# Writing the router's transposed rows to memory and reading them back as the operand of the shared expert's first six units

## The chip, the cores and the metric

One core of a Trainium2 chip runs the whole kernel in one launch. The metric is the device time in microseconds of that launch; several runs are taken and the median counts. The engines are TensorE (PE in the profile, with PEld for its weight loads), VectorE (DVE), ScalarE (ACT), GpSimd (POOL), and SyncE (SP), which only issues transfers here.

## The reference

An adaLN transformer block on x of 2 x 1024 tokens of width 512, all in float32: attention with 16 heads, then a feed-forward part. Only the second half matters here:

```python
h = _layernorm(x, axis=-1) * (1 + cb) + sb
x = x + gb * ffn(h)

def ffn(h):                                    # h: 2048 rows of 512
    topk_idx, topk_w = _route(h, router_weight, e_bias)   # logits = h @ router_weight.T, 8 of 64 experts
    moe_out = _moe_experts(h, topk_idx, topk_w, w_gate, w_up, w_down)
    return moe_out + silu(h @ sh_gate) * (h @ sh_up) @ sh_down
```

Each of the 64 experts takes up to 512/2 = 256 rows, and every row also passes the shared expert.

## The kernel before

The rows are held as 16 tiles of 128 tokens. Attention runs in chunks of two tiles. Behind each chunk, tile by tile, comes the residual and the second layer norm, whose result h (tile `h2`, two buffers) is stored to the table `h2_dram` by SP (line 592); PE transposes it (`turn`, L1189), ACT copies the transposed tile from PSUM into `h2T` (`rows_T`, L858), and PE multiplies `h2T` with the router's weights (`logits`, L1195). DVE then computes the routing in 33 small steps (`route`), and a position table by one-hot products: `hot` (L1784) and `collect` (L1793) on DVE, `weigh` on ACT (L880), `place` on PE (L1228). When all 16 tiles are placed, `finish_slots` writes the tile `slots` (L1801).

The feed-forward part is a list of units of 256 rows: six units of the shared expert in front (FRONT = 6, tiles 0 to 11), then the 64 experts, then the last two shared units. Every unit goes through the same stages:

- load of its 256 rows into one of three buffers `xg`: for shared units by SP from `h2_dram` (`load_shared`, L577), for experts by an indirect DMA of GpSimd with `slots` (`gather`, L715);
- `turn_rows` (L1314): eight PE transposes of `xg` into PSUM banks 0 and 1;
- `rows_hi` on ACT (L937): the float32r high part `x_hi` out of PSUM; `rows_lo` on DVE (L1812): the low part `x_lo`, PSUM minus `x_hi`;
- `up_first`, `up_second`, `up_third` on PE (L1328). `up_first` wants `x_hi`, `up_second` wants `x_lo`;
- `gates` on ACT (L942, L943), `hidden` on DVE (L1888, L1889), `hidden_hi` on ACT (L948, L950), `hidden_lo` on DVE (L1894, L1895), `down` on PE (L1367);
- for a shared unit `shared_out` on DVE adds the result to the residual (L1926); for an expert ACT and DVE weigh the rows and GpSimd adds them to a table in memory by indirect DMA (`add_rows`, L730).

Each engine's order is written out by hand; an engine runs its own list strictly in order and waits on semaphores. Between the end of attention and the experts' loop, DVE's list interleaves the six shared units with `route(4, n)` for the last two tiles, the last four `hot`/`collect` steps and `finish_slots`. PE's list holds `turn_shared(0)` to `turn_shared(5)` there, `up_first(2..4)` wait for `hidden` of the unit before (the first five units share PSUM banks), `up(5)` is followed by `turn_rows` of expert 0 (which waits for its gather), and from then on the loop is the same eight groups per expert.

Of the kernel before, what the change touches and what calls it, by code (L numbers as in the profile page):

```python
# [7 lines left out]
P = 128  # L8
# [3 lines left out]
KC = D // P  # L12
# [3 lines left out]
CAP = 2 * 1024 * TOPK // E  # L16
HALVES = CAP // P
# [7 lines left out]
FRONT = 6  # L25
# [3 lines left out]
RING = 3  # L29
# [30 lines left out]
def build_program(nc, x, c_t, wmod, wq_t, wkv_t, wo_t, w_pre, w_qn, w_kn, router_t, e_bias,  # L60
# [7 lines left out]
    acc_dram = [nc.dram_tensor(f"acc_dram{p}", [NTOK + EXTRA, D], f32).ap() for p in range(2)]  # L68
    rows_dram = nc.dram_tensor("rows_dram", [B, 4 * D], f32).ap()

    ctx = ExitStack()
    with ctx:
        def sem(name):
            return ctx.enter_context(nc.semaphore(name))
# [165 lines left out]
        def pair(n):  # L240
            return ps[:, 2 * n:2 * n + 2, :]
# [18 lines left out]
        s_wq, s_wkv, s_late = sem("s_wq"), sem("s_wkv"), sem("s_late")  # L260
        s_h2_out = [sem(f"s_h2_out{p}") for p in range(2)]
        s_wts, s_wts_out = sem("s_wts"), sem("s_wts_out")
        s_sh_w = sem("s_sh_w")
# [72 lines left out]
        def tile_rows(t):  # L336

            return row_view(h2_dram, t - t % TPF, TPF)[:, 0, t % TPF, 0:D]
# [169 lines left out]
        def tile_due(m, part, steps=1):  # L508
# [8 lines left out]
            return found  # L517

        def gate_bank(n, p):

            return 0 if isinstance(n, int) and n < EARLY else p
# [5 lines left out]
        def _(sp):  # L527
# [41 lines left out]
            for p in range(2):  # L569
                sp.dma_start(acc_dram[p].rearrange("(t p) n -> p t n", p=P),  # L570
                             zeros[:, 0:D].unsqueeze(1).to_broadcast([P, (NTOK + EXTRA) // P, D])).then_inc(s_init, 16)

            def load_shared(n, at):
                for p in range(2):
                    sp.wait_ge(s_h2_out[p], 16 * (n + 1))
                for h in range(HALVES):
                    sp.dma_start(xg[at % RING][:, h, 0:D], tile_rows(n * HALVES + h))\  # L577
                      .then_inc(s_xg[at % RING], 16)

            for t in range(CT * CLOSE):  # L580
                if t == CT * (CLOSE - 1):
                    sp.wait_ge(s_mm, pieces_before(NT))
                    sp.wait_ge(s_sc, 2 * steps_before(CLOSE))
                    for b in range(B):
                        sp.dma_start(gb[:, b, :], rows_dram[b, 3 * D:4 * D].unsqueeze(0).to_broadcast([P, D])).then_inc(s_gb, 16)
                    sp.dma_start(sh_gu[:, :, :], sh_gate_up).then_inc(s_sh_w, 16)
                    sp.dma_start(sh_d[:, 0, :], sh_down[0:IA, :]).then_inc(s_sh_w, 16)
                    sp.dma_start(sh_d[0:IB, 1, :], sh_down[IA:EI, :]).then_inc(s_sh_w, 16)
                    for n in range(RING):
                        load_shared(n, n)  # L590
                sp.wait_ge(s_h2, t + 1)
                sp.dma_start(tile_rows(t), h2[:, t % 2, :]).then_inc(s_h2_out[t % 2], 16)
                if t % RT == 0 and t:
                    store_weights(t // RT - 1)
# [12 lines left out]
            sp.wait_ge(s_sc, 2 * steps_before(NCHUNK))  # L607
            sp.wait_ge(s_T, RING)
            load_shared(RING, RING)
            sp.wait_ge(s_pv, steps_before(NCHUNK) // 2)  # L610
# [4 lines left out]
            for n in range(RING + 1, FRONT):  # L615
                sp.wait_ge(s_T, n)
                load_shared(n, n)
            begin, n = ROUTES[NR - 1]
# [34 lines left out]
        def _(pool):  # L653
# [30 lines left out]
            def row_rms(q):  # L684
                pool.wait_ge(s_oms, q + 1)
                inv_sqrt(orstd[:, q % 2, :], oms[:, :], CT).then_inc(s_orstd, 1)

            for m in range(FIRST * H, END):
                for q, g, kt in steps_at(m):
                    if kt >= keys(q) - CT:  # L690
                        causal(q, g, kt)
                for q in chunk_due(m, "row_rms"):
                    row_rms(q)
                for tile, _ in tile_due(m, "rstd"):
                    tile_rstd(tile)
                for tile, _ in due(m, "head_rms"):
                    head_rms(tile)
                for k, at in enumerate(STATS_AT, 2):
                    if m == at + STATS[k][1] - STATS[k][0] + 1:
                        tiles_rstd(k)  # L700
            row_rms(CLOSE)
            for t in (CT * CLOSE, CT * CLOSE + 1):
                tile_rstd(t)
            for p in range(2):
                pool.wait_ge(s_h2_out[p], 16 * (NT // 2))
# [27 lines left out]

            for e in range(RING + 1):
                gather(e)
# [7 lines left out]
        def _(act):  # L743
# [284 lines left out]
        def _(pe):  # L1028
# [273 lines left out]

            pe.sem_inc(s_T, 2)
            pe.sem_inc(s_gu, 2)
# [77 lines left out]

            def turn_shared(n):
                turn_rows(n, n % RING, s_xg, n // RING + 1)

            a, b = CT * CLOSE, CT * CLOSE + 1
            turn_shared(0)
            pe.wait_ge(s_ex, a)
# [12 lines left out]
            up_third(0, 0, sh_gu_hi, sh_gu_lo)  # L1401
            turn_shared(1)
            turn(b)
# [3 lines left out]
            up_third(1, 1, sh_gu_hi, sh_gu_lo)  # L1407
            turn_shared(2)
# [4 lines left out]
            turn_shared(3)  # L1413
            down(1, 1, sh_d_hi[0], sh_d_lo[0])
            up(3, 1, sh_gu_hi, sh_gu_lo)
            turn_shared(4)
            down(2, 0, sh_d_hi[0], sh_d_lo[0])
# [4 lines left out]
            up_third(4, 0, sh_gu_hi, sh_gu_lo)  # L1422
            turn_shared(5)
            place(15)
# [60 lines left out]
        def _(dve):  # L1485
# [429 lines left out]
            def step(n, p, expert=None, r=None):  # L1915
                hidden(n + 1, 1 - p)
                if expert is not None:
                    take_weights(expert, r)
                rows_lo(n + 2, p)
                hidden_lo(n + 1, 1 - p)  # L1920
# [9 lines left out]
            divide(CLOSE, NG - 1)  # L1930
            rows_lo(0, 0)
            hot(12, 0)
# [17 lines left out]
            hidden(0, 0)  # L1950
            rows_lo(1, 1)
            hidden_lo(0, 0)
# [7 lines left out]
            for n in range(18, COUNTED):  # L1960
                route(4, n)
            rows_lo(3, 1)
            for n in range(COUNTED, 28):
# [7 lines left out]
            hot(14, 1)  # L1971
            rows_lo(4, 0)
            shared_out(2, 2)
# [6 lines left out]
            finish_slots()  # L1980
            rows_lo(5, 1)
            hidden_lo(4, 0)
# [123 lines left out]
```

## Time and profile before

| | |
|---|---|
| median of 3 runs | 1230.19 us |
| lowest, highest | 1229.79, 1232.54 us |
| span of the profiled execution | 1233.0 us |
| busy PE / DVE / ACT / POOL | 95% / 79% / 62% / 40% |
| share of the chain that ended last, on PE | 71% |

The profiled execution's span is 2.8 us above the median. Its times stand in microseconds from the span's start. The attention part ends near 645, the six shared units in front run to 708, the experts to about 1184, and the rest is the last shared units and the final sums. Within the profile a line of code is named L1314 and so on; a busy time says how long an engine had an instruction at hand, and the bracket behind a row says how long it had been idle before, and whose result ended the idle time.

### The profile page before, as it was taken

Reading aid. Unit: us, or ns where it says so; the run is one execution under the profiler, and the core shown is the slowest. Engines: PE = TensorE matmul, PEld = TensorE weight load, DVE = VectorE, ACT = ScalarE, POOL = GpSimd, SP = SyncE. Lnnn points to the kernel's source line nnn. Section 1 sums busy time; section 2 is a strip of 40 time slices with the busy share of each in tenths; the row PEclk is TensorE's granted clock in tenths of the full one; section 3 lists DMA queues with packets and bytes.
Section 4 is the critical chain, followed back from the end, with each engine's and each line's share of the span. In section 5 each row is a group of like instructions: output and inputs, shape, how many; then the busy total and the mean of one; then the engine's idle time right before and its main releaser. Section 6 shows DMA issues by size and latency. Waiting matters only on the chain.

```text
span 1233.0 us, 25541 instructions
## 1 busy us (share of the span) xinstructions
PE 1168.1 (95%) x8905; PEld 879.7 (71%) x8905; DVE 972.6 (79%) x1881; ACT 762.0 (62%) x1507; POOL 497.9 (40%) x375
## 2 busy tenths in 40 slices
PE   8988999999999988999999999999999999999996
PEld 4455556555565655555557899999999999999982
DVE  4678776756657888775767889899888999999976
ACT  3456555555664644455564477787777887777841
POOL 1122212102122111201100148887888778788740
PEclk9999999989999998999999999999999999999999
DMA  9570000000000000003004179999999999999988
GB/s 349 172 302 1 2 18 2 10 9 2 15 10 10 9 1 22 1 10 95 29 14 141 25 225 299 289 302 302 292 295 306 299 297 296 298 301 294 298 231 290
DMA packets 75167, 189.95 MB, mean 154 GB/s; under 512 B 11544, under 2 KB 12184, under 8 KB 74832
## 3 DMA queue, kind: packets, MB, share of 16 engines
q1 hardware_dynamic: 44704, 116.27, 28.0%
q0 software_dynamic: 28672, 71.32, 23.5%
q10 hardware_dynamic: 1712, 1.32, 0.3%
q8 instruction: 48, 0.79, 0.3%
q14 instruction: 31, 0.25, 0.1%
HBM read 136.36 MB, written 52.51 MB: 153 GB/s over the span
## 4 chain that ended last, share of the span: by engine, by line
PE 71%; DVE 13%; DVEq 4%; issue 3%; DMA 3%; ACT 3%; POOL 0%; SPq 0%; POOLq 0%; ACTq 0%
PE ps L1328 22%; PE ps L1367 12%; PE ps L1147 8%; PE ps L1314 5%; PE ps L1177 4%; PE ps L1132 4%; PE ps L1060 4%; PE ps L1092 4%; DVE nmax L1610 3%; PE ps L1117 2%; DMA acc_dram<-y,slots 1%; PE ps L1032 1%; PE ps L1164 1%; DMA wq<-in_wq_t 1%; PE ps L1195 1%
## 5 line engine op out<-in xcount | busy, mean ns | idle before, releaser
L730 POOL DMA_INDIRECT acc_dram<-y,slots x128 | 252.2, 1971 | 74.1 <-issue 47.9
L1610 DVE TENSOR_REDUCE nmax<-ps 128x1 f32<-128x512 f32 (+3 forms) x304 | 191.3, 656 | 95.3 <-PE ps L1096 52.4
L839 ACT ACTIVATE probs<-ps 128x512 f32<-128x512 f32 (+1 forms) x320 | 159.0, 554 | 87.2 <-PE ps L1132 86.3
L681 POOL TENSOR_SCALAR_AFFINE_SELECT probs<-probs 128x512 f32<-128x512 f32 x64 | 44.3, 691 | 376.7 <-ACT probs L839 376.6
L715 POOL DMA_INDIRECT xg<-h_dram,slots x128 | 130.7, 1021 | 84.4 <-DVE slots L1801 40.5
L1092 PE MATMUL ps<-kpad,qpT 128*128 128x512 f32 (+3 forms) x384 | 146.7, 450 | 15.5 <-DVE nmax L1610 13.4
L1328 PE MATMUL ps<-x_hi,e_gu_hi 128*112 128x256 f32 (+1 forms) x768 | 120.1, 278 | 0.0
L1132 PE MATMUL ps<-qT,kT 98*128 98x512 f32 (+1 forms) x320 | 115.1, 437 | 5.0 <-ACT probs L839 4.8
L1328 PE MATMUL ps<-x_hi,e_gu_lo 128*112 128x256 f32 (+1 forms) x768 | 119.6, 278 | 0.0
L1812 DVE TENSOR_TENSOR e_gu_lo<-e_gu,e_gu_hi 128x1408 fp32r<-128x1408 f32 x64 | 103.8, 1622 | 11.0 <-ACT e_gu_hi L960 9.9
L1328 PE MATMUL ps<-x_lo,e_gu_hi 128*112 128x256 f32 (+1 forms) x768 | 109.9, 279 | 0.0
L1328 PEld LDWEIGHTS ps<-x_hi,e_gu_hi 128*112 128x112 f32 (+1 forms) x768 | 105.7, 179 | 5.9
L1092 PEld LDWEIGHTS ps<-kpad,qpT 128*128 128x128 f32 x384 | 67.3, 195 | 50.3 <-DVE nmax L1610 25.4
L1328 PEld LDWEIGHTS ps<-x_hi,e_gu_lo 128*112 128x112 f32 (+1 forms) x768 | 100.8, 179 | 0.0
L1328 PEld LDWEIGHTS ps<-x_lo,e_gu_hi 128*112 128x112 f32 (+1 forms) x768 | 96.0, 179 | 0.0
L1812 DVE TENSOR_TENSOR x_lo<-ps,x_hi 128x1024 fp32r<-128x1024 f32 x72 | 88.1, 1224 | 2.9 <-ACT x_hi L937 1.9
L960 ACT ACTIVATE e_gu_hi<-e_gu 128x1408 fp32r<-128x1408 f32 x64 | 88.2, 1378 | 0.1
L1367 PE MATMUL ps<-e_d_hi,hid_hi 112*128 112x512 f32 (+1 forms) x256 | 85.9, 417 | 0.0
L937 ACT ACTIVATE x_hi<-ps 128x1024 fp32r<-128x1024 f32 x72 | 73.9, 1026 | 18.5 <-PE ps L1314 18.1
L1147 PE MATMUL ps<-probs,v_sb 128*32 128x256 f32 (+1 forms) x1280 | 83.4, 380 | 0.6 <-POOL probs L681 0.6
L1367 PE MATMUL ps<-e_d_hi,hid_lo 112*128 112x512 f32 (+1 forms) x256 | 80.8, 397 | 0.0
L1147 PE MATMUL ps<-probs,ones 128*32 128x256 f32 (+1 forms) x1280 | 79.4, 367 | 0.0
(238 smaller groups left out, 2375.1 us busy)
## 6 DMA issues: line engine op xcount, KB each, us to landing
e_gu<-in_gate_up SPq DMA_DIRECT2D x64, 704.0 KB, 7.3
e_d<-in_w_down SPq DMA_DIRECT2D x64, 224.0 KB, 4.7
acc_dram<-h SPq DMA_DIRECT2D x2, 4608.0 KB, 26.0
e_d<-in_w_down SPq DMA_DIRECT2D x64, 128.0 KB, 5.4
wmod_b<-in_wmod SPq DMA_DIRECT2D x2, 2048.0 KB, 22.0
xg<-h_dram SPq DMA_DIRECT2D x16, 256.0 KB, 7.0
acc_a<-acc_dram SPq DMA_DIRECT2D x8, 512.0 KB, 10.0
acc_b<-acc_dram SPq DMA_DIRECT2D x8, 512.0 KB, 7.7
```

The costliest lines, as they stand in the source:

```text
L715: pool.indirect_dma_start(out=xg[r][:, h, :], out_offset=None, in_=h2_dram, in_offset=bass.IndirectOffsetOnAxis(ap=slots[:, at:at + 1], ax ...
L730: pool.indirect_dma_start(out=acc_dram[a], out_offset=bass.IndirectOffsetOnAxis(ap=slots[:, at:at + 1], axis=0), in_=y[e % 2][:, h, :], in ...
L839: act.activation(probs[:, n % PROBS, 2 * pr:2 * pr + 2, off:CW], unit_bank(2 * n + pr)[:, :, off:CW], ACT.Exp).then_inc(s_exp, 1)
L937: act.activation(x_hi[p][:, :, :].rearrange(flat), pair(0).rearrange(flat), ACT.Copy).then_inc(s_xa, 1)
L960: act.activation(e_gu_hi[p][:, :, :].rearrange(flat), e_gu[p][:, :, :].rearrange(flat), ACT.Copy)\
L1092: last = pe.matmul(view[:, a, :], qpT[:, t % 2, (first + a) // GH, :], kpad[:, (first + a) % GH, lo:hi], start=(a == 0), stop=(a == heads ...
L1132: pe.matmul(unit_bank(2 * n + pr)[:, :, off:CW], kT[0:QK, b, kt * P:kt * P + P], qT[q % 2][0:QK, head:head + 2, off:CW], start=True, stop= ...
L1147: last = pe.matmul(ps[HD * j:HD * j + HD, PV_BANK, at + off:at + CW], v_sb[:, b, kt, :] if at == 0 else ones[:, :], probs[:, (n + kt % 2) ...
L1328: last = pe.matmul(dst, w[:, cc, col:col + wide], rows_t[:, cc, :], start=(k == 0 and cc == 0), stop=(k == 2 and cc == KC - 1))
L1367: last = pe.matmul(ps[:, 6 + h, :], left[:, h * P:(h + 1) * P], w, start=(k == 0), stop=(k == len(products) - 1))
L1610: dve.tensor_reduce(nmax[:, 1 if lo else 0, first:first + heads], max_view(n, heads, hi - lo), AX.X, ALU.max, negate=True).then_inc(s_max, 1)
L1812: return dve.tensor_tensor(dst[:, :, :].rearrange(flat), whole[:, :, :].rearrange(flat), hi[:, :, :].bitcast(f32).rearrange(flat), ALU.sub ...
```

## The change

A third table, `turned_dram`, holds the rows of the six front units already transposed. For tiles 0 to 11, SP writes `h2T` to it right behind the store of `h2`, and `rows_T` of the next tile waits until that store has landed. `load_shared` of the six front units becomes `load_turned`: the transposed rows land in the same `xg` buffers. PE's six `turn_shared` are gone. ACT's `rows_hi` reads the buffer instead of PSUM for these units, and the low parts, six `rows_lo` of DVE, become six `turned_lo` of GpSimd with both inputs in SBUF. `turned_lo(0)` stands in GpSimd's list ahead of the last `row_rms`; `turned_lo(1..4)` after the last `tile_rstd` and ahead of the waits for the gathers; `turned_lo(5)` after `gather(0)` and `gather(1)`.

```diff
+            def load_turned(n):
+                for p in range(2):
+                    sp.wait_ge(s_turned_out[p], 16 * (n + 1))
+                for k in range(0, KC, 2):
+                    sp.dma_start(turned(n)[:, k:k + 2, :], turned_dram[n, :, k:k + 2, :]).then_inc(s_xg[n % RING], 16)
...
                 sp.dma_start(tile_rows(t), h2[:, t % 2, :]).then_inc(s_h2_out[t % 2], 16)
+                if t < TURNED:
+                    sp.wait_ge(s_h2T, t + 1)
+                    half = slice(t % HALVES * P, t % HALVES * P + P)
+                    sp.dma_start(turned_dram[t // HALVES, :, :, half], h2T[:, :, :]).then_inc(s_turned_out[t % 2], 16)
...
-            sp.wait_ge(s_T, RING)
-            load_shared(RING, RING)
+            sp.wait_ge(s_xd, 1)
+            load_turned(RING)
...
             for n in range(RING + 1, FRONT):
-                sp.wait_ge(s_T, n)
-                load_shared(n, n)
+                sp.wait_ge(s_xd, n - RING + 1)
+                load_turned(n)
...
+            def turned_lo(n):
+                pool.wait_ge(s_xa, n + 1)
+                pool.tensor_tensor(x_lo[n % 2][:, :, :], turned(n), x_hi[n % 2][:, :, :].bitcast(f32),
+                                   ALU.subtract).then_inc(s_xd, 1)
+
+            turned_lo(0)
             row_rms(CLOSE)
             for t in (CT * CLOSE, CT * CLOSE + 1):
                 tile_rstd(t)
+            for n in range(1, FRONT - 1):
+                turned_lo(n)
...
-            for e in range(RING + 1):
+            gather(0)
+            gather(1)
+            turned_lo(FRONT - 1)
+            for e in range(2, RING + 1):
                 gather(e)
...
             def rows_T(t):
                 if t:
                     act.wait_ge(s_lg, t)
+                if 0 < t <= TURNED:
+                    act.wait_ge(s_turned_out[(t - 1) % 2], 16 * ((t - 1) // 2 + 1))
...
             def rows_hi(n, p):
                 hold(act, s_gu, n + 1)
-                act.wait_ge(s_T, n + 3)
-                act.activation(x_hi[p][:, :, :].rearrange(flat), pair(0).rearrange(flat), ACT.Copy).then_inc(s_xa, 1)
+                if in_front(n):
+                    act.wait_ge(s_xg[n % RING], 32 * (n // RING + 1))
+                    act.activation(x_hi[p][:, :, :].rearrange(flat), turned(n).rearrange(flat), ACT.Copy).then_inc(s_xa, 1)
+                else:
+                    act.wait_ge(s_T, n + 3)
+                    act.activation(x_hi[p][:, :, :].rearrange(flat), pair(0).rearrange(flat), ACT.Copy).then_inc(s_xa, 1)
...
-            turn_shared(0)
...
-            rows_lo(0, 0)
```

The other five `turn_shared` of PE and the other five `rows_lo` of DVE go in the same way, each from its place in the hand-written list.

## Rows read from the trace of the kernel before

**Rows 1.** Busy time by stretch: us, then PE, PEld, DVE, ACT, POOL, clock, DMA share, GB/s.

```profile
670.00:702.00 32.00, 29.33 (x210) 26.07 (x209) 26.93 (x84) 15.25 (x31) 0.00 (x0) 1.00 0.07 19
900.00:1100.00 200.00, 200.00 (x1469) 188.06 (x1468) 182.84 (x273) 158.13 (x272) 161.74 (x109) 1.00 1.06 298
```

**Rows 2.** Chain that ended last, in order of time: start, us, what.

```profile
701.83 0.30 DVE slots L1801
...
703.10 1.19 POOL xg L715
...
704.59 3.78 DMA xg<-h_dram,slots
```

**Rows 3.** VectorE in order of time: start, us, line, operation, idle before.

```profile
673.65 0.17 DVE L1704 TENSOR_TENSOR lo<-lo 128x16 f32<-128x16 f32 x1
...
675.69 1.22 DVE L1812 TENSOR_TENSOR x_lo<-ps,x_hi 128x1024 fp32r<-128x1024 f32 x1
...
683.14 0.29 DVE L1737 TENSOR_TENSOR wts<-score,sel 128x128 f32<-128x128 f32 x1
...
685.01 1.22 DVE L1812 TENSOR_TENSOR x_lo<-ps,x_hi 128x1024 fp32r<-128x1024 f32 x1
...
691.92 0.17 DVE L1770 SCALAR_TENSOR_TENSOR col<-key,top 128x16 f16<-128x16 f32 x1
...
697.26 0.29 DVE L1793 TENSOR_TENSOR found<-found,ps 128x128 f32<-128x128 f32 x1 [0.16 <-issue]
```

**Rows 4.** ScalarE in order of time.

```profile
672.42 1.01 ACT L937 ACTIVATE x_hi<-ps 128x1024 fp32r<-128x1024 f32 x1
...
676.02 0.83 ACT L950 ACTIVATE hid_hi<-hid 64x256 fp32r<-64x256 f32 x2
...
680.59 0.37 ACT L943 ACTIVATE gact_b<-ps 64x256 f32<-64x256 f32 x1
...
689.22 0.36 ACT L943 ACTIVATE gact_b<-ps 64x256 f32<-64x256 f32 x1
```

**Rows 5.** TensorE in order of time.

```profile
695.18 1.10 PE L1228 MATMUL ps<-hot_col,hot_row 128*128 128x128 f16 x8
696.03 1.17 PE L1328 MATMUL ps<-x_lo,sh_gu_hi 128*128 128x256 f32 x8
...
704.67 1.07 PE L1328 MATMUL ps<-x_lo,sh_gu_hi 128*128 128x256 f32 x8
...
708.51 1.06 PE L1314 MATMUL ps<-con,xg 128*128 128x128 f32 x8 [1.34 <-DMA xg<-h_dram,slots]
```

**Rows 6.** GpSimd in order of time, the fourth gather behind the slots.

```profile
708.30 0.95 POOL L715 DMA_INDIRECT xg<-h_dram,slots  x1 [0.30 <-issue]
```

**Rows 7.** GpSimd's groups over the whole span, shapes apart.

```profile
L681 POOL TENSOR_SCALAR_AFFINE_SELECT probs<-probs 128x512 f32<-128x512 f32 x64 | 44.3, 691 | 376.7 <-ACT probs L839 376.6
...
L663 POOL TENSOR_TENSOR center<-center,rstd 128x4 f32<-128x4 f32 x3 | 0.6, 200 | 0.4
```

**Rows 8.** GpSimd, then VectorE, in order of time near 320 us.

```profile
318.93 0.63 POOL L681 TENSOR_SCALAR_AFFINE_SELECT probs<-probs 128x512 f32<-128x512 f32 x1 [6.89 <-ACT probs L839]
...
320.39 3.24 POOL L655 TENSOR_TENSOR rr<-ms,mhalf 128x17 f32<-128x17 f32 x1
...
316.73 0.43 DVE L1757 SCALAR_TENSOR_TENSOR marked<-score,cmp_a 128x256 f32<-128x256 f32 x1
...
319.07 0.77 DVE L1759 TENSOR_TENSOR marked<-marked,con 128x256 f32<-128x256 f32 x1
...
320.62 0.74 DVE L1667 SCALAR_TENSOR_TENSOR h<-xres,mv,mods 128x512 f32<-128x512 f32 x1
```

**Rows 9.** TensorE by stretch: us, PE busy, granted clock, DMA share, GB/s.

```profile
637.00:640.00 3.00, 0.84 (x10) 0.97 0.00 0
640.00:642.00 2.00, 2.00 (x19) 0.50 0.00 0
```

**Rows 10.** Transfers by line over the span: count, KB each, median us to landing.

```profile
h_dram<-h SPq DMA_DIRECT2D x14, 256.0 KB, 2.0
```

More of the change, by code:

```diff
@@ L69, in build_program @@
     rows_dram = nc.dram_tensor("rows_dram", [B, 4 * D], f32).ap()
+    turned_dram = nc.dram_tensor("turned_dram", [FRONT, P, KC, CAP], f32).ap()
     ctx = ExitStack()
@@ L261, in build_program @@
         s_h2_out = [sem(f"s_h2_out{p}") for p in range(2)]
+        s_turned_out = [sem(f"s_turned_out{p}") for p in range(2)]
         s_wts, s_wts_out = sem("s_wts"), sem("s_wts_out")
@@ L517, in tile_due, with turned, in_front @@
             return found
+        TURNED = FRONT * HALVES
+        def turned(n):
+            whole = xg[n % RING][:, :, :].rearrange("p h n -> p (h n)")[:, 0:KC * CAP]
+            return whole.rearrange("p (c t) -> p c t", t=CAP)
+        def in_front(n):
+            return isinstance(n, int) and n < FRONT
         def gate_bank(n, p):
@@ L615, in _ @@
             for n in range(RING + 1, FRONT):
-                sp.wait_ge(s_T, n)
-                load_shared(n, n)
+                sp.wait_ge(s_xd, n - RING + 1)
+                load_turned(n)
             begin, n = ROUTES[NR - 1]
@@ L1301, in _ @@
                     logits(tile)
-            pe.sem_inc(s_T, 2)
+            pe.sem_inc(s_T, FRONT + 2)
             pe.sem_inc(s_gu, 2)
@@ L1381, in down_last @@
                 last.then_inc(s_dn, 1)
-            def turn_shared(n):
-                turn_rows(n, n % RING, s_xg, n // RING + 1)
             a, b = CT * CLOSE, CT * CLOSE + 1
-            turn_shared(0)
             pe.wait_ge(s_ex, a)
@@ L1401, in _ @@
             up_third(0, 0, sh_gu_hi, sh_gu_lo)
-            turn_shared(1)
             turn(b)
@@ L1407, in _ @@
             up_third(1, 1, sh_gu_hi, sh_gu_lo)
-            turn_shared(2)
             pe.wait_ge(s_found, 14)
@@ L1412, in _ @@
             count(4)
-            turn_shared(3)
             down(1, 1, sh_d_hi[0], sh_d_lo[0])
             up(3, 1, sh_gu_hi, sh_gu_lo)
-            turn_shared(4)
             down(2, 0, sh_d_hi[0], sh_d_lo[0])
@@ L1422, in _ @@
             up_third(4, 0, sh_gu_hi, sh_gu_lo)
-            turn_shared(5)
             place(15)
@@ L1918, in step @@
                     take_weights(expert, r)
-                rows_lo(n + 2, p)
+                if not in_front(n + 2):
+                    rows_lo(n + 2, p)
                 hidden_lo(n + 1, 1 - p)
@@ L1950, in _ @@
             hidden(0, 0)
-            rows_lo(1, 1)
             hidden_lo(0, 0)
@@ L1961, in _ @@
                 route(4, n)
-            rows_lo(3, 1)
             for n in range(COUNTED, 28):
@@ L1971, in _ @@
             hot(14, 1)
-            rows_lo(4, 0)
             shared_out(2, 2)
@@ L1980, in _ @@
             finish_slots()
-            rows_lo(5, 1)
             hidden_lo(4, 0)
```

## The prediction

> **What bounds the kernel now.** I read the busy time by stretch first, then the chain that ended last, then each engine in order of time. From 709 us to the last units PE has no gap: in a stretch of 200 us it is busy for 200.00 [rows 1]. Whatever moves the start of this stretch moves the end by as much. It starts with PE's transposes of expert 0 at 708.51, which waited for the gathered rows [rows 5]. The chain leads back from there to GpSimd's gather at 703.10 and to DVE's `slots`, which end at 702.13 [rows 2]. So two times matter: when `slots` is ready, and how long after it PE can turn expert 0, now 708.51 - 702.13 = 6.4 us. Before that, from 670 to 702, PE is busy for 26.07 by its loads and 29.33 by its matmuls, DVE for 26.93 of 32 us [rows 1]; the chain there is almost all DVE, its routing steps and the units' parts in one list. The question is not what PE's transposes cost, but what DVE's list gains and what happens behind `slots`.
>
> **Part by part. PE's transposes** (`turn_shared`): each has a step of about 0.9 us, but PE waited after or before most of them for `hidden` or `shared_out` of DVE. They are worth only what they free: ACT's `rows_hi(1)` need not wait for them, which starts the last tile's logits and so the routing some 0.3 us earlier. Taken as -0.3.
>
> **DVE loses three `x_lo` of 1.22 us between the start of routing and `slots`.** They are not worth the same. The first at 675.69 ran to 676.9 [rows 3], and the step behind it, `hidden_lo(1)`, wants ACT's `hid_hi`, which ended at 676.02 + 0.83 = 676.85 [rows 4]: removed, it leaves a wait in its place and gains 0. The second at 685.01 [rows 3] has a routing step behind it that waits for nothing: -1.2. The third (unit 4) stands between the one-hot products and `collect(14)`; see below. `x_lo(0)` and `x_lo(1)` lie before PE's out projection and ahead of an idle wait for the logits: 0. `x_lo(5)` stood just behind `slots`.
>
> **GpSimd's subtraction, 128x1024 with two inputs in SBUF.** No row shows it. DVE does it in 1.22 [rows 3]. GpSimd's one-input select of 128x512 takes 0.69, in the undisturbed case 0.63 [rows 7, 8], and a small two-input product 0.20 [rows 7]. That gives 0.43 per 512 elements above a fixed 0.20: 1.06 if the second input cost nothing, 1.9 with a second stream of inputs, and 2.5 if all of the select's 0.63 is counted four times. I take 1.9, since a second stream of the same length is the nearest that the rows support. The Trainium skill (GPSIMD Engine Reference, section "Performance versus the Vector engine") measures 4497 ns for the same kind of operation at 2048 elements, which as an estimate would be 2.25 us here; no run here shows it, and by it the forecast would be 1.0 to 1.5 us later.
>
> **What DVE pays for it.** Beside the select at 318.93 to 319.56, DVE's two-input step at 319.07 took 0.77, where the same width at 316.73 took 0.43 [rows 8]: it waited until GpSimd was through. Against it, DVE's step at 320.62 kept its 0.74 beside a GpSimd operation of 3.24 that reads only 17 elements [rows 8]. So the exclusion lasts as long as GpSimd reads, and 1024 elements are read for nearly the whole 1.9 us. The routing steps are small two-input steps, all from SBUF, so I follow each of the three:
> - `turned_lo(2)` starts when ACT's `x_hi` ends, 673.43 [rows 4], less the 0.3: 673.1. DVE stands then at the step of 673.65 [rows 3], a two-input one: it loses 1.9. Shift of DVE's list: -0.3 + 1.9 = +1.6.
> - `turned_lo(3)`: ACT's gates end at 680.96 [rows 4]; with the shift and 1.0 for `x_hi` the subtraction runs from 683.6 to 685.5. DVE reaches the two-input step of 683.14 [rows 3] at 684.7 and waits 0.7. Shift +2.3, and -1.2 for the removed `x_lo(3)`: +1.1.
> - `turned_lo(4)`: gates end at 689.58 [rows 4]; PE is still late by 1.6, so it runs from about 692.2 to 694.1. DVE reaches the step of 691.92 [rows 3] at 693.0 and waits 1.1: +2.2. With this shift `place(14)` on PE goes from 695.18 to 697.4; its successor came 0.85 later [rows 5], so `collect(14)` can run at 698.35 where it ran at 697.26 [rows 3]: +1.1. The removed `x_lo(4)` is what allows this. `place(15)` and `hidden(4)` follow with the same shift.
>
> `slots` is then ready at 702.13 + 1.1 = 703.2. The Trainium skill states this exclusion (SBUF — State Buffer, section "Who interferes with whom": a DVE instruction with two SBUF inputs contends with a GpSimd instruction that reads SBUF, and the second to issue blocks fully). It speaks against this change. By it, as by the row of 0.77, the slots are 1.1 later; without it they would be earlier by 2.2 (next part but one).
>
> **Behind `slots`: the step that decides.** `turned_lo(5)` is behind four gather issues in GpSimd's list. The fourth ended at 708.30 + 0.95 = 709.25 [rows 6], 7.1 us after `slots`. Then come the 0.3 that stands between two GpSimd instructions [rows 6], 1.9 for the subtraction and 0.1 for the handover: `x_lo(5)` is there 9.4 us after `slots`. PE has `up_first(5)` done by then and stands at `up_second(5)`. From there to the end of the unit's products it took 708.51 - 1.34 - 704.67 = 2.5 [rows 5]. So expert 0 is turned 11.9 us after `slots`, where it was 6.4: +5.5. The gathered rows, which ended the wait before, landed 704.59 + 3.78 - 702.13 = 6.2 us after `slots` [rows 2] and have long been there. Everything behind (gathers 2 and 3, `add_rows`) has experts of time.
>
> **The clock.** `up_second(5)` ran 704.67 - 702.13 = 2.5 us after `slots` [rows 5]; with 9.4 in its place PE idles some 6.9 us. After a gap of about 2 us (busy 0.84 of 3.00 from 637) the granted clock was 0.50 from 640 to 642 [rows 9], that is 1.2 instead of 2.4 GHz, with PE fully busy. I take that the same follows here and lasts about 3.4 us, a bit longer than this row: half of it is lost, +1.7; between 0 and 3.4.
>
> **The rest.** Twelve more stores of 256 KB in the attention part: a store lands in 2.0 us [rows 10], the next tile's `rows_T` comes many microseconds later, and the DMA engines are nearly idle there; 0, or up to 1 if the added waits in ACT's list cost 0.1 each. `turned_lo(0)` ahead of `row_rms`: the residual waits for PE's out projection anyway, 0. Loads of units 3 to 5 are asked for earlier than they were needed: 0.
>
> **Sum.** +1.1 (slots) + 5.5 (behind slots) + 1.7 (clock) = +8.3. Against the profiled span of 1233.0 that is 1241.3; the span is 2.8 above the median, and the difference goes to the median: 1230.2 + 8.3 = 1238.5 us.
>
> **Rivals.**
> - A, the above: 1238.5, between 1235.5 (subtraction 1.5, no clock loss) and 1241 (subtraction 2.25, more clock). Chance 0.55.
> - B, DVE isn't held by GpSimd. For it speaks the step of 0.74 beside the long operation [rows 8]. Then the list has only -0.3, 0, -1.2, and behind `place(14)`, which now is 1.5 earlier, another -0.7 because `x_lo(4)` is gone: slots -2.2, total -2.2 + 5.5 + 1.7 = +5.0, 1235.2; without clock loss 1233.5. Chance 0.2.
> - C, the other side, faster: GpSimd gives the gathers to its descriptor work and takes up the subtraction at once, so that `x_lo(5)` is ready before the gathered rows land. It decides from 6.4 - 2.5 = 3.9 us behind `slots`. Then only B's gain is left: -2.2, 1228.0. Against it: each GpSimd instruction started 0.30 after the last one's end [rows 6], none beside it. Chance 0.06.
> - D, worse: the subtraction takes 2.5 or more, as DVE and GpSimd hold each other, and the slow clock lasts 6.8 us. Slots +2.4, behind them +6.1, clock +3.4: +11.9, 1242.1. Chance 0.13.
> - E, C's overlap with A's losses on DVE, or the change hidden for another reason: about 1230. Chance 0.06.
>
> **How the numbers follow.** The likeliest is A, 1238.5. Range 1232.8 to 1242.5: it takes B whole, A whole, and most of D, and leaves C and E out. Faster by over 0.2% (2.5 us, about what a measurement of this kernel can tell from no change) is only a part of C: 0.04; within it are the rest of C, E and a little of B: 0.10; slower 0.86.
>
> **What would show it.** In the profile after: GpSimd's `x_lo` of five units with 1.5 to 2.3 us each, and DVE's two-input routing steps of 0.17 to 0.29 us lengthened to about 2 beside them (A) or not (B); `slots` near 703; PE idle for 6 to 7 us ahead of an L1328 row on `x_lo,sh_gu_hi`, released by POOL, and a clock of 0.50 behind it; turns of expert 0 near 715 to 717; all behind shifted by one constant. Wrong it would be if PE's wait ahead of that row were short: then GpSimd's order does not hold the subtraction back, and the sum loses its largest term.

## The result, and the profile after

The changed kernel takes 1241.15 us in the median (1237.56 to 1241.83). The ratio to the kernel before is 1.0075, with an interval of 1.0061 to 1.0089: slower by 9.2 us, between 7.5 and 11.0 (the two medians differ by 11.0). One further run of the kernel before took 2864.72 us, a slow one, and is in neither the ratio nor the profiles. The profiled execution took 1239.94 us, with a span of 1238.2. Forecast were 1238.5 us and a loss of 8.3 us, from two places: `slots` 1.1 later (1.4 if counted from the routing's first step, as below), and expert 0 turned 7.2 later behind them. The two places are right. The sizes are not: the first cost 4.0 and the second 6.5.

Its busy times over the whole span, from the first part of the page:

```profile
PE 1163.8 (94%) x8857; PEld 876.6 (71%) x8857; DVE 974.4 (79%) x1875; ACT 761.9 (62%) x1507; POOL 511.2 (41%) x381
```

GpSimd has gained 1 point of share and nothing stands out. The loss doesn't show in shares. By stretch of the new kernel (columns as in [rows 1]) it does:

```profile
670.00:702.00 32.00, 24.57 (x156) 22.17 (x155) 25.39 (x70) 11.35 (x25) 7.11 (x3) 0.89 0.06 19
709.00:720.00 11.00, 8.71 (x49) 8.27 (x50) 3.05 (x7) 3.98 (x7) 4.78 (x4) 0.71 0.49 160
900.00:1100.00 200.00, 200.00 (x1468) 188.06 (x1467) 182.44 (x272) 158.34 (x272) 161.59 (x109) 1.00 1.06 297
```

The expert part is as it was: 200.00 of 200 us on PE, as in [rows 1]. In the routing stretch PE has 4.8 us less of busy time, of which its four transposes (`turn_shared`, 1.03 to 1.07 us each, overlapping their neighbours) make some 4. The matmul clock is 0.89 where it was 1.00, and GpSimd, which did nothing there, is busy for 7.11 with three instructions. These are GpSimd's instructions in order of time (as [rows 6]; three subtractions, the first gathers, the last subtraction):

```profile
670.12 2.34 POOL L726 TENSOR_TENSOR x_lo<-xg,x_hi 128x1024 fp32r<-128x1024 f32 x1 [5.17 <-ACT x_hi L974]
682.19 2.41 POOL L726 TENSOR_TENSOR x_lo<-xg,x_hi 128x1024 fp32r<-128x1024 f32 x1 [9.73 <-ACT x_hi L974]
689.50 2.37 POOL L726 TENSOR_TENSOR x_lo<-xg,x_hi 128x1024 fp32r<-128x1024 f32 x1 [4.91 <-ACT x_hi L974]
703.64 1.19 POOL L746 DMA_INDIRECT xg<-h_dram,slots  x1 [11.77 <-DVE slots L1832]
705.13 0.97 POOL L746 DMA_INDIRECT xg<-h_dram,slots  x1 [0.30 <-issue]
706.41 1.20 POOL L746 DMA_INDIRECT xg<-h_dram,slots  x1 [0.30 <-issue]
707.92 0.95 POOL L746 DMA_INDIRECT xg<-h_dram,slots  x1 [0.30 <-issue]
708.89 2.35 POOL L726 TENSOR_TENSOR x_lo<-xg,x_hi 128x1024 fp32r<-128x1024 f32 x1
```

A subtraction takes 2.34 to 2.41 us, not 1.9. The last one starts only when the fourth gather is issued. VectorE beside them, to be held against [rows 3]:

```profile
667.16 0.23 DVE L1718 TENSOR_SCALAR biased<-ex 128x128 f32<-128x128 f32 x1 [1.60 <-ACT ex L902]
...
670.22 2.26 DVE L1735 TENSOR_TENSOR lo<-lo 128x16 f32<-128x16 f32 x1
...
675.64 0.43 DVE L1925 TENSOR_TENSOR hid_lo<-hid,hid_hi 112x256 fp32r<-112x256 f32 x1 [1.21 <-ACT hid_hi L990]
...
682.21 2.53 DVE L1768 TENSOR_TENSOR wts<-score,sel 128x128 f32<-128x128 f32 x1
...
691.35 0.55 DVE L1797 TENSOR_SCALAR top<-key 128x16 f32<-128x16 f32 x1 [0.43 <-issue]
...
697.65 0.29 DVE L1824 TENSOR_TENSOR found<-found,ps 128x128 f32<-128x128 f32 x1 [1.37 <-PE ps L1268]
...
702.37 0.29 DVE L1832 SCALAR_TENSOR_TENSOR slots<-found,spare 128x128 int32<-128x128 f32 x1
...
705.14 1.65 DVE L1843 TENSOR_TENSOR e_gu_lo<-e_gu,e_gu_hi 128x1408 fp32r<-128x1408 f32 x1 [0.26 <-issue]
```

The step that took 0.17 at 673.65 [rows 3] takes 2.26, and the one that took 0.29 at 683.14 [rows 3] takes 2.53. Each ends where the subtraction beside it ends (672.46 and 684.60; the steps at 672.48 and 684.74). Such a step is called held below: it ends only when GpSimd's instruction has. TensorE, to be held against [rows 5]:

```profile
674.48 1.22 PE L1368 MATMUL ps<-x_hi,sh_gu_hi 128*128 128x256 f32 x4 [4.20 <-DVE hid L1920]
...
690.58 0.74 PE L1407 MATMUL ps<-sh_d_hi,hid_hi 112*128 112x512 f32 x2 [2.78 <-DVE xres L1958]
...
711.29 2.08 PE L1368 MATMUL ps<-x_lo,sh_gu_hi 128*128 128x256 f32 x8 [6.07 <-POOL x_lo L726]
...
715.56 1.03 PE L1354 MATMUL ps<-con,xg 128*128 128x128 f32 x8
```

PE has three long waits, 4.20, 2.78 and 6.07 us. The same eight products that took 1.07 in [rows 5] take 2.08 after the last wait. The granted clock says why; PE by stretch in the new kernel (us, PE busy, clock, DMA share, GB/s):

```profile
674.70:678.10 3.40, 3.40 (x18) 0.54 0.14 53
691.80:695.20 3.40, 3.40 (x13) 0.55 0.01 2
703.00:708.80 5.80, 2.22 (x18) 0.98 0.43 118
709.00:715.70 6.70, 4.41 (x22) 0.53 0.78 257
```

Behind each of the three waits there is a stretch at half clock (1.2 instead of 2.4 GHz), two of 3.4 us and one that covers what is left of unit 5. The kernel before has none between 645 and 709.

**Where the time went**, with the end of the routing's first step (`biased<-ex`) as a mark: 670.83 before (its row starts at 670.60 and takes 0.23) and 667.39 after.

| us | before | after | difference |
|---|---|---|---|
| first routing step ends | 670.83 | 667.39 | -3.44 |
| from there to the end of `slots` | 31.29 | 35.27 | +3.98 |
| from `slots` to expert 0 turned on PE | 6.39 | 12.90 | +6.51 |
| sum: expert 0 turned | 708.51 | 715.56 | +7.05 |

Of the -3.44, 3.2 arose in the attention part: its last marker, DVE's `sel_b`, ended at 639.79 before and at 636.58 after. Experiment 4 speaks against these 3.2 belonging to the change. From that marker to the turn of expert 0 the change costs 10.3 us, which lies inside the interval of the timed runs. The 7.05 by which the experts start later is kept to the final sums, whose first product on PE starts at 1208.53 against 1201.50. The span shows only 5.2 of it, because the profile of before took 10.7 us from PE's last product to its end, this one 8.9, and the experiments' 8.8 to 10. The distances between the marks repeat better than the spans do: experiment 4 leaves this part as it was and has 31.32 and 6.41 us for the second and third line of the table.

### The profile page after: what moved, and what is told of

Its sections match the earlier page's. It is cut to its first block, busy times and chain, and to the rows that moved or that the text cites. A ratio compares the mean times of both kernels' runs of the same rounds, so it can differ in the third digit from the quotient of the medians.

```text
span 1238.2 us, 25451 instructions
## 1 busy us (share of the span) xinstructions
PE 1163.8 (94%) x8857; PEld 876.6 (71%) x8857; DVE 974.4 (79%) x1875; ACT 761.9 (62%) x1507; POOL 511.2 (41%) x381
## 4 chain that ended last, share of the span: by engine, by line
PE 73%; DVE 13%; DVEq 4%; issue 3%; ACT 3%; DMA 2%; POOL 1%; SPq 0%; POOLq 0%; ACTq 0%
PE ps L1368 23%; PE ps L1407 13%; PE ps L1187 8%; PE ps L1354 5%; PE ps L1217 4%; PE ps L1100 4%; PE ps L1172 4%; PE ps L1132 4%; DVE nmax L1641 3%; PE ps L1157 2%; PE ps L1072 1%; PE ps L1204 1%; DMA wq<-in_wq_t 1%; PE ps L1235 1%; ACT probs L873 1%
## 5 line engine op out<-in xcount | busy, mean ns | idle before, releaser
L1843 DVE TENSOR_TENSOR x_lo<-ps,x_hi 128x1024 fp32r<-128x1024 f32 x66 | 80.8, 1225 | 1.5 <-ACT x_hi L977 0.7
L982 ACT ACTIVATE gact_a<-ps 112x256 f32<-112x256 f32 x72 | 27.7, 384 | 88.2 <-PE ps L1368 88.2
```

Of the source, the lines that this page charges most:

```text
L1843: return dve.tensor_tensor(dst[:, :, :].rearrange(flat), whole[:, :, :].rearrange(flat), hi[:, :, :].bitcast(f32).rearrange(flat), ALU.sub ...
```

## The experiments

My theory: the loss has two causes that add up. GpSimd's place for unit 5, behind four gather issues, costs expert 0 its start; GpSimd's reading beside DVE's two-input steps costs the routing. Against it stood: that GpSimd's slowness alone is the cause (no exclusion), that the new stores to memory cost time, and that only the wait behind `slots` counts.

**Experiment 1: unit 5's subtraction ahead of the wait for `slots`.**

```diff
-            for n in range(1, FRONT - 1):
+            for n in range(1, FRONT):
                 turned_lo(n)
...
-            gather(0)
-            gather(1)
-            turned_lo(FRONT - 1)
-            for e in range(2, RING + 1):
+            for e in range(RING + 1):
                 gather(e)
```

> The changed kernel with one step moved: GpSimd's low part of unit 5 stands ahead of the waits for the slots, no longer behind four gather issues. Theory (the recorded prediction's largest term is GpSimd's order): the wait of 6.1 us ahead of up_second(5) goes, and the slow clock behind it; expert 0 is turned 6.4 to 7.5 us after the slots instead of 12.9, so the whole is 5.5 to 6.5 us faster than the changed kernel, about 1234. Rival (DVE's lost time in the routing is the main term, the wait merely absorbs it): under 2 us gained, still about 1239. GpSimd takes the subtraction at 701.5 to 703.9, so the first gather may start 0.3 later.

Measured: 1240.05 us (1239.07 to 1242.60), ratio 1.0066 (1.0041 to 1.0091). PE's wait ahead of `up_second(5)` is gone, and still almost nothing is won. The time is the rival's (about 1239), but not for the rival's reason. Its GpSimd, then DVE, then PE:

```profile
703.49 2.41 POOL L726 TENSOR_TENSOR x_lo<-xg,x_hi 128x1024 fp32r<-128x1024 f32 x1 [9.56 <-ACT x_hi L971]
...
708.89 2.30 POOL L746 DMA_INDIRECT xg<-h_dram,slots  x1 [0.30 <-issue]
...
703.90 2.15 DVE L1827 SCALAR_TENSOR_TENSOR spare<-found,spare 128x128 f32<-128x128 f32 x1
...
708.72 1.62 DVE L1840 TENSOR_TENSOR e_gu_lo<-e_gu,e_gu_hi 128x1408 fp32r<-128x1408 f32 x1 [0.26 <-issue]
...
706.96 1.07 PE L1365 MATMUL ps<-x_lo,sh_gu_hi 128*128 128x256 f32 x8
...
715.46 1.94 PE L1351 MATMUL ps<-con,xg 128*128 128x128 f32 x8 [6.01 <-DMA xg<-h_dram,slots]
```

The subtraction now runs while DVE makes `spare`, the step ahead of `slots`: 2.15 us instead of 0.29. So `slots` end 36.96 us behind the first routing step (35.27 in the changed kernel). Then the second gather's issue falls beside DVE's `e_gu_lo` and takes 2.30 instead of 0.97, and expert 0 is turned 9.0 behind `slots`. PE's wait is only moved, from `x_lo` to the gathered rows, and is 6.01 long; the products behind it are slow again (1.94 us instead of 1.06). From the routing's first step to the turn of expert 0, 46.0 us pass, against 48.2 in the changed kernel and 37.7 before. My expectation missed since I had placed this subtraction in a free time of DVE.

**Experiment 2: all six low parts on DVE, at the places where the kernel before has them, read from the loaded rows.** GpSimd has none; PE's transposes stay away, the stores stay in.

```diff
-            turned_lo(0)
...
-            for n in range(1, FRONT - 1):
-                turned_lo(n)
...
             def rows_lo(n, p):
+                if in_front(n):
...
+                    dve.wait_ge(s_xa, n + 1)
+                    dve.wait_ge(s_xd, n)
+                    dve.tensor_tensor(x_lo[p][:, :, :], turned(n), x_hi[p][:, :, :].bitcast(f32), ALU.subtract).then_inc(s_xd, 1)
+                    return
```

> The changed kernel, but all six low parts are made by DVE at the places of the kernel before, with both inputs in SBUF; GpSimd makes none. Transposes stay removed. Theory (both losses come from GpSimd: the exclusion in the routing and its order behind the slots): DVE's routing steps are back at 0.17 to 0.29 us, slots come 31.2 to 31.5 us after the routing's first step (35.5 in the changed kernel), expert 0 is turned 6.4 us behind the slots; total 1229 to 1230.5, like the kernel before or up to 1 us faster. Rival (removing PE's transposes, reading x_hi from SBUF, or the stores cost the time): over 1233.

Measured: 1229.08 us (1227.49 to 1232.90), ratio 0.9983 (0.9968 to 0.9998); a second time, beside other runs of before, 1228.93, ratio 0.9987 (0.9971 to 1.0003), where a ratio of 0.998 to 0.9995 was expected. The whole loss is gone. DVE there, around the place of the held step:

```profile
670.41 0.18 DVE L1730 TENSOR_TENSOR lo<-lo 128x16 f32<-128x16 f32 x1
...
672.45 1.21 DVE L1912 TENSOR_TENSOR x_lo<-xg,x_hi 128x1024 fp32r<-128x1024 f32 x1
673.74 0.42 DVE L1927 TENSOR_TENSOR hid_lo<-hid,hid_hi 112x256 fp32r<-112x256 f32 x1
```

The step is short again. The subtraction from SBUF takes DVE 1.21, as from PSUM [rows 3], and `hidden_lo(1)` follows without a wait: this subtraction costs nothing, as the prediction had it, for in the changed kernel the same `hid_lo` waits 1.21 for ACT's `hid_hi` (675.64, above). `slots` come 30.92 behind the first step and the turn 6.46 behind `slots`; before it was 31.29 and 6.39, and the second profile of this kernel has 30.91 and 6.47. So the rows from memory, without PE's transposes, are worth 0.4 us ahead of `slots`; the timed runs alone hardly tell this gain from none.

**Experiment 3: unit 5 alone back to DVE, behind `slots`; units 0 to 4 on GpSimd.** The `rows_lo` of experiment 2, for n = 5 only, and the gathers in one loop.

> The changed kernel, but DVE makes the low part of unit 5 right behind the slots, as the kernel before; GpSimd makes units 0 to 4. Theory: the same gain as with GpSimd's step moved ahead: no wait of PE behind the slots, 5.5 to 6.5 us off the changed kernel, and what is left over the kernel before, 3 to 4.5 us, is the exclusion in the routing: 1233 to 1235. Rival (no exclusion, the long steps of 2.26 and 2.53 in the trace are something else and would be hidden): 1229 to 1231.

Measured: 1235.07 us (1232.33 to 1236.86), ratio 1.0028 (1.0016 to 1.0040), at the upper end of what was expected. `slots` to turn: 6.4, as before. First step to `slots`: 35.11, as in the changed kernel. Its DVE:

```profile
669.58 2.26 DVE L1735 TENSOR_TENSOR lo<-lo 128x16 f32<-128x16 f32 x1
...
681.46 2.53 DVE L1768 TENSOR_TENSOR wts<-score,sel 128x128 f32<-128x128 f32 x1
...
690.59 0.65 DVE L1797 TENSOR_SCALAR top<-key 128x16 f32<-128x16 f32 x1 [0.42 <-issue]
```

The same three steps are held. The two causes are apart now: the one behind `slots` is worth the way from this kernel to the changed one, 1.0075 - 1.0028, some 5.8 us; the one ahead of `slots` the way from experiment 2 to this kernel, 1.0028 - 0.9983, some 5.5 us. By the intervals each is uncertain by some 2 us. By the profiles it is 6.5 and 4.2 (35.11 - 30.92).

**Experiment 4: the kernel before with the changed kernel's stores and ACT's waits for them, and nothing else.** What is stored is read by nobody.

```diff
+                if t < TURNED:
+                    sp.wait_ge(s_h2T, t + 1)
+                    half = slice(t % HALVES * P, t % HALVES * P + P)
+                    sp.dma_start(turned_dram[t // HALVES, :, :, half], h2T[:, :, :]).then_inc(s_turned_out[t % 2], 16)
```

> The kernel before with one part of the change alone: the transposed rows of tiles 0 to 11 are also stored to memory, and ACT's copy of the next tile waits for the store; nothing reads them. Theory: 0, at most 1 us, since the stores land in 2 us on idle transfer engines: 1229.5 to 1231. Rival: each store or the wait delays ACT in attention, or shifts where the clock falls: 1232 or more, or 1228 or less, with the attention part longer or shorter in the trace (in the changed kernel's profile it was 3.2 us shorter).

Measured: 1232.09 us (1229.38 to 1233.41), ratio 1.0001 (0.9988 to 1.0013). The stores cost nothing that shows within 1.5 us. The median alone lies in the rival's band, but the runs of before beside it had 1231.03. Its profiled execution reached the marker `sel_b` at 636.28, 3.5 us earlier than the profile of before, while the timed runs don't differ. The ten profiles of kernels with these stores besides it have this marker between 636.0 and 638.7, without a change to the attention part among them. So about 3 us of this part vary from one execution to another, and the profile of before is a long one; what makes them vary stays open, and there is only one profile without the stores.

**Experiment 5: unit 2's subtraction done twice on GpSimd**, to weigh the exclusion by itself.

```diff
+                if n == 2:
+                    pool.tensor_tensor(x_lo[n % 2][:, :, :], turned(n), x_hi[n % 2][:, :, :].bitcast(f32), ALU.subtract)
+                    pool.drain()
```

> The changed kernel with GpSimd's low part of unit 2 computed twice, one after the other (the first has no reader). Theory (a GpSimd operation that reads two tiles from SBUF holds DVE's two-input steps for as long as it runs): the long step of 2.26 us at the routing's twelfth instruction stays, and a second DVE step, the next one or the one after it, is lengthened to about 2.3 us too, so hidden(1) and the slots come about 2.2 us later than in the changed kernel (37.5 to 38 us behind the routing's first step, against 35.5). Rival (the 2.26 is a delay of its own kind, such as a semaphore or an instruction fetch at this place): one long step only, slots unchanged.

Measured: 1241.88 us, one run. GpSimd, then DVE:

```profile
669.69 2.34 POOL L727 TENSOR_TENSOR x_lo<-xg,x_hi 128x1024 fp32r<-128x1024 f32 x1 [5.17 <-ACT x_hi L977]
672.17 2.34 POOL L729 TENSOR_TENSOR x_lo<-xg,x_hi 128x1024 fp32r<-128x1024 f32 x1
...
669.80 2.26 DVE L1738 TENSOR_TENSOR lo<-lo 128x16 f32<-128x16 f32 x1
672.13 0.18 DVE L1740 TENSOR_TENSOR lo<-lo,mid 128x16 f32<-128x16 f32 x1
672.38 2.16 DVE L1742 TENSOR_TENSOR gsum<-hi,lo 128x16 f32<-128x16 f32 x1
```

Two subtractions, two held steps, and one DVE step, begun in the 0.14 us between them, keeps its usual 0.18. `slots` come 36.56 behind the first step, 1.3 later than in the changed kernel instead of the 2.2 to 2.7 that I expected: the later subtractions then meet DVE elsewhere, and not all of a held step reaches `slots`.

**Experiment 6: two fills of `x_lo` by GpSimd ahead of unit 2's subtraction.** Is it GpSimd's being busy that holds DVE, or its reading?

```diff
+                if n == 2:
+                    for _ in range(2):
+                        pool.memset(x_lo[n % 2][:, :, :].bitcast(f32), 0.0)
+                        pool.drain()
```

> The changed kernel with two memsets of the same tile by GpSimd, 0.95 us each as the kernel before has one, right ahead of its low part of unit 2, which then starts about 2.2 us later. Theory (it is GpSimd's reads that hold DVE): beside the memsets DVE's two-input steps keep their 0.17 to 0.29 us, and the long step appears only when the subtraction begins, further on in the routing or at hidden_lo. Rival (any GpSimd instruction on SBUF holds DVE, writes too): steps of 0.9 us and more already beside the memsets.

Measured: 1238.85 us, one run. GpSimd (the two fills in one row), then DVE:

```profile
669.54 2.03 POOL L728 MEMSET x_lo<- 128x1024 f32 x2 [5.16 <-ACT x_hi L978]
671.71 2.39 POOL L730 TENSOR_TENSOR x_lo<-xg,x_hi 128x1024 fp32r<-128x1024 f32 x1
...
669.66 0.18 DVE L1739 TENSOR_TENSOR lo<-lo 128x16 f32<-128x16 f32 x1
...
672.99 1.39 DVE L1929 TENSOR_TENSOR hid_lo<-hid,hid_hi 112x256 fp32r<-112x256 f32 x1 [1.22 <-ACT hid_hi L994]
```

Beside the fills, DVE's two-input step keeps 0.18. Beside the subtraction that follows, `hid_lo` takes 1.39 instead of 0.43 and ends 0.3 behind it (674.38 and 674.10). So neither GpSimd's being busy nor its writes hold DVE. What the subtraction has and the fills lack is reads from SBUF, and the exclusion goes with them. One run doesn't tell this kernel's time from the changed one's.

**Experiment 7: experiment 2 with units 3 and 4 on GpSimd**, where DVE was said to lose least and gain 1.2 twice. Edit: `rows_lo` returns for n in (3, 4), and GpSimd has `turned_lo(3)` and `turned_lo(4)`.

> The version in which DVE makes the front units' low parts, but GpSimd makes those of units 3 and 4, the two that stood in DVE's way: each removes 1.22 us from DVE's list. Theory (exclusion by the remaining GpSimd time): each costs DVE's next two-input step 1.0 to 1.2 us, so the two nearly cancel; within 0.5 us of the version with all on DVE, 1228.6 to 1229.6, slots 30.7 to 31.7 us behind the routing's first step against 31.2. Rival (only the long step in unit 2 mattered, the others are free): 1.5 to 2 us faster than it, about 1227.

Measured: 1231.16 us (1229.61 to 1234.76), ratio 1.0011 (0.9998 to 1.0023), against 0.9983 of experiment 2: by the ratios some 3 us lost, by the medians 2, with intervals that just touch, where I expected a tie. GpSimd, then DVE:

```profile
680.06 2.39 POOL L727 TENSOR_TENSOR x_lo<-xg,x_hi 128x1024 fp32r<-128x1024 f32 x1 [19.07 <-ACT x_hi L971]
688.93 2.38 POOL L727 TENSOR_TENSOR x_lo<-xg,x_hi 128x1024 fp32r<-128x1024 f32 x1 [6.49 <-ACT x_hi L971]
...
681.47 1.13 DVE L1765 TENSOR_TENSOR wts<-score,sel 128x128 f32<-128x128 f32 x1
...
689.10 2.25 DVE L1796 TENSOR_SCALAR top<-top 128x16 f32<-128x16 f32 x1
```

The second held step reads one array only, 128x16, and takes 2.25 us. It ends with the subtraction (691.35 and 691.31). My rule for DVE, two inputs in SBUF, was too narrow. Unit 4's subtraction met such a step early in its 2.38 us, and the PE that waits for it then was at half clock: `slots` 33.35 behind the first step, 2.4 later than in experiment 2.

**Experiment 8: the changed kernel, with matmuls that fill PE's three waits** (17, 10 and 25 products of a constant array, 128x512, into a bank of PSUM that nobody reads then). It tells what the clock costs by itself.

```diff
+            def fill(k):
+                for _ in range(k):
+                    pe.matmul(ps[:, 0, :].rearrange("p (a k) -> p a k", k=P), ones_b[:, :], ones_b[:, :].unsqueeze(1).to_broadcast([P, 4, P]), start=True, stop=True)
...
+            up_first(FRONT - 1, 1, sh_gu_hi, sh_gu_lo)
+            fill(25)
+            up_second(FRONT - 1, 1, sh_gu_hi, sh_gu_lo)
```

> The changed kernel with products of ones that nobody reads, 17, 10 and 25 of them, ahead of the three places where PE waited 4.2, 2.8 and 6.1 us. Nothing else changes. Theory (part of the loss is the clock of 1.2 GHz behind these waits): no stretch at 0.50 between 670 and 720, unit 2's products take 4.6 instead of 6.0 us, the products behind the last wait 2.4 instead of 4.3; 2.5 to 4 us off the changed kernel, 1236 to 1238. Rival (the slow clock falls into stretches where PE waits anyway): under 1 us gained, 1239 to 1241.

Measured: 1238.63 us (1238.29 to 1239.27), ratio 1.0069 (1.0052 to 1.0086), a little over the 1236 to 1238 expected. PE in it, in order of time:

```profile
674.47 0.74 PE L1368 MATMUL ps<-x_hi,sh_gu_hi 128*128 128x256 f32 x4 [0.52 <-DVE hid L1929]
...
710.44 1.19 PE L1368 MATMUL ps<-x_lo,sh_gu_hi 128*128 128x256 f32 x8 [0.69 <-POOL x_lo L726]
...
712.89 1.03 PE L1354 MATMUL ps<-con,xg 128*128 128x128 f32 x8
```

The products behind the first and the last wait are back at 0.74 and 1.19, from 1.22 and 2.08. Expert 0 is turned at 712.89, 2.7 earlier, with the routing's first step at the same time (667.38 and 667.39): 0.85 of it ahead of `slots`, 1.8 behind. The medians differ by 2.5, but the two kernels were timed beside different runs of before, and the ratios' intervals overlap; so the clock's 2.7 rest on the profiles. One stretch of half clock is left, near 682, behind a wait of PE of 1.21 us, so ahead of `slots` 0.85 is not all that the clock can cost.

**Experiment 9: experiment 2 with two low parts earlier.** `rows_hi(2)` on ACT and `rows_lo(2)` go into DVE's wait for the routing's logits (2.41 us in experiment 2), `rows_lo(3)` to the place where `rows_lo(2)` was free. One DVE step of 1.2 us then leaves the way from the first step to `slots`.

```diff
             hidden(0, 0)
+            rows_lo(1, 1)
             hidden_lo(0, 0)
+            rows_lo(2, 0)
             for n in range(10):
                 route(4, n)
-            step(0, 0)
+            hidden(1, 1)
+            rows_lo(3, 1)
+            hidden_lo(1, 1)
```

> The version with all front low parts on DVE, with two steps made earlier, which only the rows read from memory allow, since they need no PSUM bank: ACT makes x_hi of unit 2 ahead of the last logits_out and DVE its x_lo in the 2.4 us in which it waits for the logits; x_hi and x_lo of unit 3 take the place where unit 2's stood, the 1.2 us in which DVE waits for hid_hi. So no x_lo is left in DVE's chain between the routing's first step and hidden(3). Theory (a low part costs nothing in a wait and 1.2 us in the chain): slots 29.9 to 30.1 us behind the routing's first step (31.15 with all on DVE at the old places), 1.0 to 1.4 us less in all, about 1228. Rival (PE's up(3), or ACT's list, is late next): under 0.4 us gained.

Measured: 1228.03 us (1226.44 to 1231.41), ratio 0.9971 (0.9957 to 0.9985): faster than the kernel before by 3.6 us (1.8 to 5.3) and the lowest median of all here. The runs of before beside it spread from 1227.83 to 1234.78, wider than elsewhere. Its DVE, then PE:

```profile
664.88 1.23 DVE L1916 TENSOR_TENSOR x_lo<-xg,x_hi 128x1024 fp32r<-128x1024 f32 x1 [0.33 <-ACT x_hi L969]
666.93 0.23 DVE L1717 TENSOR_SCALAR biased<-ex 128x128 f32<-128x128 f32 x1 [0.83 <-ACT ex L897]
...
687.89 0.42 DVE L1925 TENSOR_TENSOR hid<-gact_a,ps 112x256 f32<-112x256 f32 x1 [0.74 <-ACT gact_b L978]
...
678.72 1.19 PE L1406 MATMUL ps<-sh_d_hi,hid_hi 112*128 112x512 f32 x2 [1.20 <-DVE xres L1963]
```

The wait for the logits is down to 0.83, so the early subtraction is hidden. `slots` come 30.57 behind the first step, 0.35 earlier than in experiment 2 and not 1.2, the gain that the rival had (under 0.4). Up to `hidden(3)` DVE is the expected 1.15 earlier; then `hidden(3)` waits 0.74 for ACT's gates, and so for PE. PE is late because its products behind the wait of 1.20 run at half clock here (0.50 from 680 to 682): unit 1's `down` takes 3.93 us from its start to that of unit 3's products, in experiment 2, behind a wait of the same 1.20, it takes 2.41. So the half clock takes back most of what is missing. No run here shows what is left once it is gone. Beside experiment 2 run again with it (0.9987) the gain is 1 to 2 us, with intervals that overlap.

## Why the prediction was right, and where it wasn't

**What bounds the kernel: right.** PE is full from the turn of expert 0 on, before and after, and the two marks, `slots` and the turn, carry the whole result.

**The removed `x_lo`: right.** Set against the first routing step, the removal of `x_lo(2)` gained nothing, `x_lo(3)` gave 1.2 (DVE's lag went from 4.75 to 3.51), and `x_lo(4)` gave 0.9, since `collect(14)` was then bound by PE's product alone (its row waits 1.37 for PE).

**The subtraction, 1.9: too small.** In every kernel here they took 2.3 to 2.4. It was right to bound it by 2.5; the value in the middle was chosen by counting the second input at the price of the first, and the upper bound was nearer. The Trainium skill's figure (GPSIMD Engine Reference, section "Performance versus the Vector engine"), 2.25 as an estimate, was nearer too; the measured 2.37 decides.

**The exclusion: right in kind, mis-sized in two of three terms.** This is the step that failed. The prediction had 1.9, 0.7 and 1.1 us for units 2, 3 and 4 (by its own start at 673.1 and end at 675.0 the first comes to 1.5); the held steps measured lost 2.1 (2.26 - 0.17), 2.2 (2.53 - 0.29) and 0.4 (0.55 - 0.17, behind a gap of 0.43 where 0.1 is usual), and the last of them was not on the path to `slots`. Unit 3 went wrong by a mechanism that I had left out. PE waits for `hidden` of DVE; when DVE is held for 2.1 us, this wait is 4.20 us, where it was 1.12 before and 2.10 in experiment 7 (without PE's transposes and without this hold), and PE's products behind it run at half clock (1.22 for four, above). So ACT's gates and `x_hi(3)` come later still, and the subtraction starts at 682.19, in the very moment in which DVE reaches its two-input step at 682.21. I had it starting 1.1 us ahead of DVE. Unit 4 was cheap since DVE had work with an operand in PSUM and a `MAX8` beside the subtraction, and came to a step that can be held only 0.5 us ahead of its end. What it lost didn't reach `slots`: PE's work ahead of `place(14)` had begun at 690.58, before the held step, and ran without a gap to 696.43, while the last input of `place(14)`, ACT's `weigh`, was ready at 695.39. Half clock behind the wait of 2.78 then stretches PE's work ahead of `place(14)` (690.58 to 696.43 is 5.85 us; before, the same work took 4.67 from 690.51 to 695.18 [rows 5]): +1.2. In sum: +2.1 for unit 2, +0.4 in which DVE waits longer for ACT and PE ahead of unit 3's step, +2.2 and -1.2 for unit 3, +1.2 for the half clock, -0.9 for the removed `x_lo(4)` and +0.15 for a last wait for ACT's gates are the 3.98 that are measured, against the 1.4 that the prediction had between these marks (+1.1, and 0.3 for the earlier start).

**Behind `slots`: right.** Forecast were 9.4 us to `x_lo(5)` and 11.9 + 1.7 = 13.6 to the turn by the full clock term (5.5 + 1.7 behind 6.4); measured are 8.6 (711.25 - 702.66) and 12.9. The third gather took 1.20 instead of the 2.13 that stood in the kernel before, and the subtraction followed the fourth gather by 0.03, not by 0.3: 1.2 less. The subtraction's 2.35 gave 0.4 back. PE's wait was 6.07 (forecast 6.9), and the clock behind it cost 1.8 by experiment 8 (forecast 1.7).

**The clock: right behind `slots`, missing ahead of it.** I had asked for one wait only. There were three. The 3.4 us of half clock that the prediction counted with fit the stretch in the trace of before near 640, of which its row shows the first 2 us: the granted clock is 0.50 up to 643 and 0.88 from 643 to 644.

**The stores, the loads, `turned_lo(0)`: right**, 0 by experiment 4. **PE's transposes:** 0.3 forecast, 0.4 in experiment 2.

**The rivals.** B (DVE isn't held) fell by experiment 5 and by the held steps. C (the subtraction passes the gathers) fell by PE's wait of 6.07. D is the closest by the median (1242.1 against 1241.15), A by the ratio (8.3 against 9.2); of D's terms the subtraction of 2.5 and more was not there, and slots +2.4 is still too small. The errors had opposite signs, 2.6 too little ahead of `slots` and 0.7 too much behind them, and the 10.3 of the profiles against 8.3 is what is left. So that the forecast of 1238.5 lies only 2.7 under the median is in part luck: the two errors work against each other.

**Open:** which of DVE's instructions are held. Beside unit 4's subtraction (689.50 to 691.87) two steps of the new kernel passed with the times that they had before: `xres`, with an operand in PSUM (1.29), and `key`, a `MAX8` of one input (0.35); the one-input `TENSOR_SCALAR` behind them was held. The runs don't show what tells the last two apart.

## What to carry to other kernels

Work given to GpSimd is not free because GpSimd is idle: ask which instructions of DVE lie beside it, since each that it holds loses the rest of GpSimd's read, and what stands ahead of it in GpSimd's own list. If the held engine feeds PE on a path without slack, count PE's wait and the half clock behind it too. Measure the parts apart before giving up a change: here the rows from memory were worth a little, and only the new engine for the low parts cost time, so that the same rows with the low parts on DVE, and one of them in a wait, beat both kernels (experiment 9, by 0.15 to 0.43% against the kernel before).

## What the runs showed that I had not expected

- GpSimd's exclusion reaches DVE instructions with one input: `TENSOR_SCALAR` of 128x16, 0.17 us alone, took 2.25 in experiment 7. It doesn't come with GpSimd's writes: two fills of 128x1024 (2.03 us) left DVE's steps at 0.18.
- The gather's issue on GpSimd is lengthened in its turn by DVE. The gather that starts while DVE's `e_gu_lo` runs (128x1408, two inputs, 1.62 to 1.65 us) took 2.13 before, 1.20 after, 2.30 in experiment 1 and 2.11 or 2.12 in experiments 2, 3, 4, 7 and 9, other gathers 0.95 to 1.21; the one that started 0.01 us ahead of `e_gu_lo` (705.13 in the changed kernel) kept its 0.97. The lengthened one ends 0.8 us behind `e_gu_lo` each time: before, 707.99 against 707.17; after, 707.61 against 706.79; in experiment 1, 711.19 against 710.34.
- A wait of PE of 2.8 us was followed by 3.4 us at half clock just as one of 4.2 was; after one of 6.07 all that was left of the unit, some 4.4 us, ran so. The wait's length alone doesn't decide: one of 1.70 in experiment 7 and one of 1.20 in experiment 9 were followed by such a stretch, and those of 1.20, 1.49 and 2.10 in experiment 2 were not.
